# Edge counts of the first 6656 destinations as a dense matrix, multiplied in layers two and three of a four-layer graph network

## What is computed

```
h = relu(layernorm(x)); x = x + L0(h)    # GCN: sums over edges by source, a 64x64 product
h = relu(layernorm(x)); x = x + L1(h)    # message MLP per edge, sum by destination, GRU
h = relu(layernorm(x)); x = x + L2(h)    # GIN:  S2 = segment_sum(h[src], dst); MLP((1+eps) h + S2)
h = relu(layernorm(x)); x = x + L3(h)    # SAGE: S3 = segment_sum(h[src], dst); relu(S3/cnt @ Wl + b + h @ Wr)
```

## Time and profile before

| | |
|---|---|
| device time, median of 3 runs | 9328.82 us (9328.22 to 9331.21) |
| span of the profiled execution | 9329.2 us |
| TensorE matmuls busy | 4953.4 us, 53% |
| VectorE busy | 3646.5 us, 39% |
| ScalarE busy | 1659.2 us, 18% |
| GpSimd busy | 6576.3 us, 70% |
| moved by DMA | 476.52 MB, mean 51 GB/s |
| granted TensorE clock, mean | 0.558 of full speed |

### The profile page before, as it was taken

One profiled execution on the slowest core, in us unless ns is written; L12 is line 12 of the kernel. 1 busy time (PEld: TensorE's weight loads), 2 busy tenths in 40 slices (PEclk: granted clock), 3 DMA queues, 4 the chain that ended last, 5 costly groups with the idle time before them and its releaser, 6 DMA issues. The chain is left out here.

```text
span 9329.2 us, 145773 instructions
## 1 busy us (share of the span) xinstructions
PE 4953.4 (53%) x31445; PEld 4537.8 (49%) x31446; DVE 3646.5 (39%) x7396; ACT 1659.2 (18%) x4731; POOL 6576.3 (70%) x6906
## 2 busy tenths in 40 slices
PE   6888888888676666666665222222223222222223
PEld 5777777777566666666665222222223222222223
DVE  9888888888544333333334111111113111111112
ACT  4455555555431000000002000000001000000000
POOL 3677777777426777777775777777774777777777
PEclk6666666666655555555556555555556555555555
DMA  8222222122442222222211111111111111111111
GB/s 328 53 55 55 54 55 55 54 55 54 156 151 59 42 42 43 42 42 43 42 41 27 27 27 27 27 27 27 27 27 32 27 27 27 27 27 27 27 27 37
DMA packets 528946, 476.52 MB, mean 51 GB/s; under 512 B 366105, under 2 KB 370347, under 8 KB 526812
## 3 DMA queue, kind: packets, MB, share of 16 engines
q0 software_dynamic: 212608, 218.99, 11.2%
q1 hardware_dynamic: 314328, 254.96, 9.6%
q10 hardware_dynamic: 1925, 1.58, 0.1%
HBM read 332.70 MB, written 142.29 MB: 51 GB/s over the span
## 5 line engine op out<-in xcount | busy, mean ns | idle before, releaser
L1270 POOL DMA_INDIRECT h_rows<-h_tab,idx x3322 | 3135.8, 944 | 1114.5 <-issue 1011.4
L1825 PE MATMUL ps_seg<-hot,h_rows 128*64 128x80 f32 x6656 | 987.0, 343 | 3024.2 <-DMA h_rows<-h_tab,idx 2950.9
L1825 PEld LDWEIGHTS ps_seg<-hot,h_rows 128*64 128x64 f32 x6656 | 895.9, 227 | 3134.5 <-issue 2282.1
L917 POOL DMA_INDIRECT sorted_tab<-msg,row_at x1661 | 1591.3, 958 | 660.5 <-issue 496.0
L1270 POOL DMA_INDIRECT a_rows<-a_tab,idx x1661 | 1567.9, 944 | 534.7 <-issue 505.1
L1752 DVE TENSOR_TENSOR acc_t<-acc_t,ps_seg 64x80 f32 x416 | 95.6, 230 | 3025.3 <-PE ps_seg L1825 3025.3
L807 PE MATMUL ps_at<-next_at,lo_t 128*128 128x98 f32 x3328 | 1032.5, 406 | 326.3 <-ACT next_at L870 276.6
L807 PEld LDWEIGHTS ps_at<-next_at,lo_t 128*128 128x128 f32 x3328 | 759.4, 282 | 378.1 <-issue 219.3
L835 PE MATMUL ps_msg<-u_win,hot_t 128*128 128x64 f32 x3328 | 830.6, 345 | 7.7 <-DVE hot_t L740 7.7
L1441 PE MATMUL ps_seg<-hot,act_rows 128*65 128x80 f32 x3328 | 492.2, 341 | 635.7 <-ACT act_rows L1514 635.7
L1441 PEld LDWEIGHTS ps_seg<-hot,act_rows 128*65 128x65 f32 x3328 | 448.9, 229 | 682.2 <-issue 682.2
(11 more groups left out here) (226 smaller groups left out, 7301.1 us busy)
## 6 DMA issues: line engine op xcount, KB each, us to landing
sorted_tab<-acc_t SPq DMA_DIRECT2D x16, 4030.0 KB
landed_rows<-sorted_tab SPq DMA_DIRECT2D x124, 520.0 KB
lo_row<-lo_tab SPq DMA_DIRECT2D x209, 256.0 KB
h_rows<-h_tab,idx POOLq DMA_INDIRECT x3322
ends_of<-edge_t SPq DMA_DIRECT2D x208, 132.0 KB
sorted_tab<-msg,row_at POOLq DMA_INDIRECT x1661
a_rows<-a_tab,idx POOLq DMA_INDIRECT x1661, 2.4
idx<-src_steps SPq DMA_DIRECT2D x624, 4.0 KB, 1.6
```

The source lines that it names most:

```text
L917: pool.indirect_dma_start(sorted_tab[:, :], bass.IndirectOffsetOnAxis(ap=row_at[:, r, k:k + 1], axis=0), msg[:, r, k, :], None).then_inc(s ...
L1270: pool.indirect_dma_start(dest[:, r, k, :], None, table[:, :], bass.IndirectOffsetOnAxis(ap=idx[:, r, k:k + 1], axis=0)).then_inc(landed[r ...
L1825: last = pe.matmul(ps_seg[0:F, b, 0, 0:W], rows_of[:, r, k, :], hot[:, b, k, :], start=(k == 0), stop=(k == K - 1))
```

## The change

The change has three parts. `JU` is 98, the chunks that hold nodes; `DSTEP` comes to 32, `KEYS` to 392, `DENSE` to 6656, `BLOCKS` to 13, `TURNS_A` to 24 and `FIRST_A` to 28.

**A stage that plans (new, between layer zero and layer one).** VectorE packs each edge into a record of two float32: the low seven bits of the source, and a code made of the destination and the source's chunk. Records go to `rec_tab` in device memory. For every group of four consecutive destinations below 6656 (1664 groups), the place in the sorted list at which its edges begin is counted: 14 indirect transfers of 4 KB rows bring the lists, and 14 pairs of compare and sum run over 1024 columns. A flag says if no group has more than 128 edges and if all edges with destinations below 6656 lie before a set step; it decides between dense and gathered work at run time. With these inputs (some 17 edges a node) it is set, and what follows is told for that case.

**In layer one's edge stage, each step also makes 32 columns of the matrix.** SyncE loads eight sets of records, each at an address that it first reads from `starts`; VectorE makes one-hots of the low bits and of the key (chunk, destination); TensorE multiplies them, eight products with 392 columns; ScalarE copies each out of PSUM as bfloat16; one transfer of 784 KiB stores them in `adj_tab` (208 of them, 167 MB). `ps_seg` has one buffer where it had two.

**In the edge stages of layers two and three, 104 pieces of the matrix replace 108 of the 208 steps.** h is split once into three bfloat16 parts (high and middle in `upper`, which takes the place of `x_nm`; low in `low`), x being saved to and brought back from device memory. ScalarE loads a piece at a time (12 or 13 chunks of sources x 512 destinations, four buffers); TensorE runs 24 or 26 matmuls of 512 columns for a piece into one bank, `ps_dense`; after eight pieces VectorE adds the bank to `acc_t`. Gathers remain for 100 steps: 96 that start at step 112 run beside the pieces, two pieces a step in the first eight and one a step in the other 88, and then steps 108 to 111. `acc_t` now holds partial sums in all 128 partitions, and the weights that read it are doubled along the rows.

```diff
+WORD = 4
+GPS = 8
+DSTEP = WORD * GPS
+KEYS = JU * WORD
...
+DENSE = SUPERS * DSTEP
...
+DCOLS = 512
+BLOCKS = DENSE // DCOLS
+PIECES = 8
+RD = 4
+UNITS_A = BLOCKS - 1
+TURNS_A = 2 * UNITS_A
+FIRST_A = TURNS - TURNS_A
+TURNS_R = 1
...
+        adj_tab = nc.dram_tensor("adj_tab", [SUPERS, P, JU * DSTEP], BF16).ap()
```

The planning stage, VectorE's larger operations and the indirect loads:

```diff
+                    step(dve.tensor_tensor(below[:, :, :], base_all[:, None, 0:SUPERS].to_broadcast([P, TC, SUPERS]),
+                                           limit[:, :, None].to_broadcast([P, TC, SUPERS]), ALU.is_lt))
...
+                    for c in range(TC):
+                        dve.wait_ge(near_in[c % RING], 16 * (c // RING + 1))
+                        dve.tensor_scalar(near_below[:, c % 2, :], near[:, c % RING, :], limit[:, c:c + 1], None,
+                                          ALU.is_lt).then_inc(near_counted, 1)
+                        dve.wait_ge(near_counted, c + 1)
+                        step(dve.tensor_reduce(step_n[:, 2, c:c + 1], near_below[:, c % 2, :], AX_X, ALU.add))
```

Layer one (SyncE, VectorE, TensorE, ScalarE in this order; products 4 to 5 stand ahead of `spread`, 6 to 7 behind it):

```diff
                             sp.dma_start(ends_w[0:W, r, :], b_tab[bass.ds(base, W), :]).then_inc(win_in[r], 16)
+                            hold(sp, lo_hot, s - RING + 1)
+                            hold(sp, keyed, s - RING + 1)
+                            for k in range(GPS):
+                                at = sp.value_load(starts[0:1, bass.ds(s * GPS + k, 1)], min_val=0, max_val=N_EDGES)
+                                sp.dma_start(rec[:, r, k, :], rec_tab[bass.ds(at, P), :]).then_inc(rec_in[r], 16)
...
+                    def group_keys(i, r):
...
+                        dve.wait_ge(rec_in[r], 16 * GPS * i + 16 * GPS)
+                        hold(dve, adj_done, GPS * (s - 1))
+                        dve.scalar_tensor_tensor(out=key_of[:, b, :], in0=rec[:, r, :, 0],
...
+                        dve.tensor_tensor(one_lo[:, b, :, :], ps_iota[:, 0:1, :].to_broadcast([P, GPS, P]),
+                                          rec[:, r, :, 1:2].to_broadcast([P, GPS, P]), ALU.is_equal).then_inc(lo_hot, 1)
...
                             one_hots(b, rel[:, b, :]).then_inc(hot_ready, 1)
+                            group_keys(i, r)
+                            group_columns(i, r, 0)
...
                             relate(1 - b, s + 1)
+                            group_columns(i, r, 1)
...
+                            pe.matmul(ps_adj[:, k % 2, 0:KEYS], one_lo[:, b, k, :], one_key[:, b, k, :], start=True,
+                                      stop=True).then_inc(adj_done, 1)
...
                                 sum_by_node(1 - b, s - 1)
+                                groups(1 - b, s - 1, 0, 2)
...
+                                groups(1 - b, s - 1, 2, 4)
...
+                            nc.scalar.activation(adj[:, b, :, k * WORD:(k + 1) * WORD],
+                                                 ps_adj[:, k % 2, 0:KEYS].rearrange("p (j d) -> p j d", d=WORD),
+                                                 ACT.Copy).then_inc(adj_kept, 1)
```

Layers two and three:

```diff
-                        gather_rows(pool, layer, table, rows_of, landed, seg_done)
+                        for i in first_then_loop(pool, TURNS_A):
+                            for r in range(RING):
+                                gather(r, i)
+                        for i, steps in rest(pool):
...
+                            act.dma_start(pieces[:, slot, :, 0:e.stop - e.start],
+                                          adj_tab[bass.ds(n * DCHUNKS, DCHUNKS), :, e].rearrange("c p e -> p c e")
+                                          ).then_inc(piece_in[slot], 16)
...
+                            for j in range(low_end, high_end):
+                                e = slice((j - low_end) * DSTEP, (j - low_end + 1) * DSTEP)
+                                pe.matmul(out_of[:, :, :], upper[:, j, :], pieces[:, slot, :, e], start=(j == 0),
+                                          stop=False, skip_group_check=True)
...
+                                last = pe.matmul(out_of[0:F, :, :], low[:, j, :], pieces[:, slot, :, e], start=False,
+                                                 stop=(j == JU - 1), skip_group_check=True)
...
+                        pe.wait_ge(split_low, len(parts))
+                        for u in first_then_loop(pe, UNITS_A):
+                            for t in range(PIECES):
...
+                                for g in piece_numbers(u, t):
+                                    multiply(u, g, t)
+                                products(q, FIRST_A * RING + q, r, i, t % 2)
```

More of the change, by code:

```diff
@@ L1251, in _, with gather_rows @@
                             norm.root(act, CHUNKS - 1)
[L1253 to L1262, removed]
+        def gather_rows(pool, table, dest, landed, used):
             for i in first_loop_last(pool, TURNS):
@@ new lines, in _ @@
+                        if layer == 2:
+                            add_own(TURNS_A, RING * TURNS_A)
+                            dve.wait_ge(x_back, 16)
+                            dve.tensor_tensor(x_nm[:, :, :], x_nm[:, :, :], ps_bias[:, 0:1, :].to_broadcast([P, J, F]),
+                                              ALU.add).then_inc(bias_added, 1)
+                        for i, steps in rest(dve):
+                            for r in range(RING):
+                                q, s, b = RING * TURNS_A + RING * i + r, steps[r], r % 2
+                                start_step(q, s, b)
+                                accumulate(q, s, b)
@@ L1828, in _ @@
-                                with pe.If(more > 0):
-                                    seen = before(pe, s)
-                                    with pe.Fori(0, more) as w:
-                                        hold(pe, segx_hot, seen + w + 1)
-                                        for k in range(K):
-                                            last = pe.matmul(ps_seg[0:F, b, 0, 0:W], rows_of[:, r, k, :], hot[:, b, k, :],
-                                                             start=(k == 0), stop=(k == K - 1))
-                                        last.then_inc(segx_done, 1)
@@ L1836, in _ @@
-                                pe.drain().then_inc(seg_done, 1)
+                                for g in piece_numbers(u, t):
+                                    multiply(u, g, t)
+                                products(q, FIRST_A * RING + q, r, i, t % 2)
+                        turn_own(TURNS_A)
+                        if layer == 3:
+                            own_terms(TURNS_A)
+                        for i, steps in rest(pe):
+                            for r in range(RING):
+                                products(RING * TURNS_A + RING * i + r, steps[r], r, TURNS_A + i, r % 2)
```

594 lines of the change are left out of this document (480 added, 114 removed).

## The result

The changed kernel takes 8188.01 us (median of 4 runs, 8185.06 to 8191.17), the one before 9330.01 beside it (9328.22 to 9338.11): a ratio of 0.8775, 95% interval 0.8762 to 0.8787. The profiled execution has a span of 8189.1 us, 1140.1 less than before. The measured time also lies 38 us above 8150, the upper end of the range.

A forecast was written before the change was run, and what follows sets the result against it. GpSimd's gathers were taken to bound the three edge stages, at 9.99 us a step. 9329 - 2038 (layers two and three) + 291 (layer one, bound by SyncE) + 70 (planning) = 7652 us, range 7400 to 8150.

The forecast's parts named there:

- SyncE's price in layer one: Layer one's edge stage: SyncE's added record work makes a step 11.35 us, above 9.99; +291 us in all.
- Eight times ... with the gaps between instructions 1.05 us: SyncE in layer one: each of eight records a step costs 1.05 us, between bounds 0.95 and 1.71.
- a step is 2.95 + 8.4: Layer one on SyncE: 2.95 us fixed with two satisfied waits, 8.4 for eight records; 11.35 us a step.
- Its rings are four deep, which hides latency, not throughput: Layer one: GpSimd also waits when SyncE's next indices stand behind eight records, since its four-deep rings hide only latency.
- Rival 3: Layer one: records dearer, or four engines waiting in turn; 13 to 14 us a step, 8000 to 8200 us; 13%.
- Rival 1: Layer one not bound by SyncE; TensorE's 10.5 us binds, 7475 us, or 7370 with no loss; 17%.
- Layers two and three: Edge stages: 861 gathers fewer a layer, -1074 us, +20 TensorE pace, +35 head and end; both -2038 us.
- the 20 us for TensorE's pace: Layers two and three: TensorE's clock balance makes a step 10.2 us rather than 9.99, +20 us a layer.
- Rival 2: Layers two and three: TensorE at the lower clock, 13.6 us a step, 8386 us in all; 9%.
- Rival 4: Layers two and three: the pieces' reads so slow (85 GB/s) that the kernel is slower than before; 2%.
- longer runs are not slower per byte: Pieces' reads in layers two and three: 768 or 832 byte runs move at least 215 GB/s, so transfers stay hidden.
- The planning stage: New stage, covered by nothing: at most 53 us of VectorE columns, 17 of short operations and round trips; +70 us.

## Why the prediction was wrong

**The step that failed is SyncE's price in layer one.** The mechanism was as predicted: layer one became bound by SyncE, GpSimd waited for `idx` in every step and VectorE for `rec` in 110 of 177. The size was not. "Eight times ... with the gaps between instructions 1.05 us" measured 1.30, and "a step is 2.95 + 8.4" left out the loop's end altogether. The fixed part was right: 3093.19 - 3080.08 = 13.11 us for the shortest step, less 8 x 1.26 for its records, leaves 3.0. The two satisfied waits in it, put at 0.05 us, last 0.017 each and, with their gaps, take 0.15 (at 3108.4 us). The 847.9 us by which the stretch from first to last gather grew are made of the 283 forecast, 204 x 8 x 0.25 = 408 for the record, 51 x 2.9 = 148 for the turns' ends, and 9 that I don't account for. The 8 us forecast behind the last gather came to 16. Four runs show it: fewer loads, no records, fewer turn ends, records elsewhere.

**Why the record was mis-sized.** Its instructions were in the rows, and their sum was not far off, 0.99 forecast and 0.90 measured; the load even fell from 0.438 to 0.269. The 0.05 for gaps was a guess. The rows held a better figure: the upper bound, 1.71 us from `ends_w` to `idx`, held a branch, a division and these same gaps, and I took a value next to the lower bound. The issues with their small register work stood 0.61 and 0.58 apart, for an issue of 0.363 and 0.09 of register work; that is 0.13 to 0.16 of gaps for two or three instructions, and seven instructions at that rate give 0.4. The measured gaps are 0.27; with the 0.10 of the one long load in a step, which no row of before showed, they come near that 0.4 by luck. The loop's end was hidden in the trace of before, since SyncE had waits in each step.

**"Its rings are four deep, which hides latency, not throughput"** held.

**Rival 3**, whose span of 8000 to 8200 holds the result, named two mechanisms as one. Only the first, dearer records, is shown. The waits in turn are refuted as the bound by the run without records and the run with half of the loads: with all products and additions in place the step falls to 10.0 and 10.4 us, where waits in turn would have kept it near 13. Rival 1's other half was right in one way: without SyncE the stage is at GpSimd's 10.0 us, not at TensorE's 10.5.

**Layers two and three** came within 34 us of 2038. The gathers kept their price beside 186 GB/s: 1033.2 us from first to last of 800 are, to 2 us, 799 x 1.248 and the 37.5 us wait for TensorE. So the 20 us for TensorE's pace were not paid, the head cost 37.5 to 39.6 rather than 30, and the 5 behind it came as forecast (5.1 from last gather to next first one in layer two, none in layer three). Rival 2 did not come: the first twelve products, behind 64 us without one, ran at 367 ns and the next at 232 (427 and 213 had been worked out for the two levels),

```profile
6021.60 4.40 PE L2269 MATMUL ps_dense<-pieces,x_nm 128*128 128x512 bf16 x12 [63.84 <-DVE low L2146]
6025.93 2.78 PE L2273 MATMUL ps_dense<-pieces,low 128*64 128x512 bf16 x12
```

and the clock was 0.88 over the stage. The clock in the records is 0.50 or 1.00 and nothing between. At 0.50 a product of 512 columns starts 0.427 us behind the one before it, at 1.00 0.216 (medians of 436 and of 4399 pairs in the changed kernel), which is 1.20 and 2.37 columns a ns; so the 427 and 213 ns, worked out with 1.2 and 2.4 GHz, came true, 213 to 3 ns. After the 64 us without a product the clock was 0.50 from 6022 to 6024 us and 1.00 from 6026 on. In layer two TensorE waited for gathered rows 54 times and 145 us at a clock of 0.88; with half of the products it waited 345 us at 0.76, and in the run with more products it had no such wait and the clock was 0.96. These runs differ in TensorE's work as well as in its waits, so they do not show which of the two moved the clock. Rival 4 is refuted by 64% of the DMA in use and gathers at an unchanged 944 ns. That longer runs are not slower per byte could not be read from the earlier trace rows, which has one rate, of packets of mostly 1024 bytes (1805 with 1.85 MB) and not of 256; the pieces' reads show it for their length: from 6302 to 6304 us of the changed kernel the DMA moved 374 GB/s, nearly all of it the pieces' 0.71 MB in 859 packets.

**The planning stage** cost 68 us of 70, though the first gather of layer one stands at 2897.0 to 2915.7 us in the runs above, so a match to 2 us is luck. VectorE worked in it from 2735.4 to 2798.1 us, 62.7 us. Its passes over columns took 44.6 us, under the bound of 53. Integers were indeed faster where they were shifted, masked or copied: 2048 columns in 1.23 us, 0.60 ns a column (the trace of before has the same on line 463, 1.226 us), and compared: 1024 in 0.75 us, 0.73 ns. Two operations that joined two inputs were not (2048 columns in 2.29 us, 1.12 ns), nor were the sums: 1024 columns in 1.22 us, 1.19 ns, and 2912 in 3.19, 1.09 ns. The 0.3 us for a short operation and the round trip of a transfer stood in none of the rows, but are in the trace of before: from 242.40 us six short dependent operations of VectorE start 0.31 us apart, and the indices of layer one land 1.6 us behind their issue (median, line 1309), so the term is 40 x 0.3 + 3 x 1.6 = 17, an estimate in which 40 and 3 are guesses. The changed kernel has 18.1 us there, 62.7 - 44.6: 29 short operations of 0.13 to 0.44 us, thirteen of them from 2793.00 us on 0.32 apart, one copy of 1.0 us, two waits for transfers, 4.3 and 4.8 us, and two for TensorE, 1.2 and 0.4.

## What to carry to other kernels

Price a queue's instructions by the interval between two of them in a row of the trace (1.30 us for a record here), never by the sum of their durations (0.90), and add the loop's end (2.9 us a turn here). Work given to an engine that idles is free only as long as its whole list of instructions, waits aside, is shorter than the step; sum that list first, then share the issues among the engines (SyncE and ScalarE here), and put each where its engine waits anyway. When every engine waits for another, a wait that can be moved at no gain is a symptom; the bound is the engine whose list, made shorter, makes the time shorter. And when added work costs something else than its sum, look where in the stage it did: here it was in the eight steps of the head, not in the steps in general.

## What the runs showed of the hardware that I had not expected

- SyncE's instructions had gaps of some 0.04 us each (0.27 us over seven), and grouping the loads did not remove them.
- In the loop, one of the eight loads in every step that was read one by one took 0.91 to 0.96 us in place of 0.27. With the loads grouped, one issue took 0.93 in place of 0.33 in one of the two steps read. The four steps written out have no such stop. The cause is open.
- The end of a loop on SyncE cost 2.9 us a turn, seen once in four steps and, with a longer body, once in eight.
- A load of one word from on-chip memory took 0.269 us here (median) and 0.438 in the rows before.
- The same kind of record costs 1.10 us in code written out and 1.30 in a loop; address arithmetic explains 0.09 of it, the one long instruction of a step the other 0.10.
- The granted clock rose with TensorE's work in layer two: 0.50 before, then 0.76, 0.88 and 0.96 with 1274, 2548 and 3822 products of 512 columns. Layer one did not order so (3200 to 4900 us): 0.75 without records, TensorE busy 76% of the time, and 0.64 with four records on ScalarE, busy 78%.
